# Splitting the scores of a half-step: one block of other TensorE work moved between the two groups of head pairs

## The chip, the cores and the metric

The kernel runs on one core of one Trainium2 chip. The metric is the device time of one execution in microseconds; the times shown are medians of several executions. Profile times are microseconds from the start of the profiled span.

## What is computed

A recurrent block and a stack of six local attention layers run on the same normalised input, and their product is added to the input. Cut to what matters here:

```python
for i in range(DEPTH):                      # 6 layers, x is (2, 1024, 128)
    x = attn_layer(shift_tokens(x), Wqkv[i], q_scale[i], k_scale[i], Wo[i]) + x
    x = ffn_layer(shift_tokens(x), ln_g[i], ln_b[i], W1[i], b1[i], W2[i], b2[i]) + x

# attn_layer: 16 heads of 64, l2-normalised and rotated q and k, windows of 32 tokens
sim = jnp.einsum('bhwie,bhwje->bhwij', bq, bk2) * QK_SCALE      # the scores
attn = jax.nn.softmax(jnp.where(mask, -big, sim), -1)
out = jnp.einsum('bhwij,bhwje->bhwie', attn, bv2)

# ffn_layer: xn is the layer norm of its input
hg = xn @ W1 + b1                           # the up product, 341 values and 341 gates
a, gate = jnp.split(hg, 2, -1)
return a * jax.nn.gelu(gate, approximate=False) @ W2 + b2

# outside: x + recurrent(layernorm(x)) * silu(attention stack(layernorm(x)))
```

## The kernel before

The two sequences of the batch are two streams, b = 0 and b = 1. The 1024 tokens of a stream are eight tiles of 128, and six layers of eight tiles make 48 steps. Each step has two half-steps, one per stream. The steps are written out one after the other, and each engine has its own function `half(i, b)` that lists what it does in half-step (i, b), strictly in that order; engines meet through semaphores alone.

The work is a software pipeline: in step i the projections (`qkv`) are those of tile i, the transposes of queries and keys and the scores are those of tile i-1, the softmax's probabilities, their product with the values and the output projection those of tile i-2, and the feed-forward part's up product that of tile i-4. Its normalised rows are transposed (`transpose_rows`) for tile i-3. In the last steps (40 to 47) the recurrent branch runs along. After step 47 a drain with an order of its own finishes what is under way.

TensorE writes to banks of PSUM in rings of two: `ps_qn` for projections, `ps_tr` for transposes, `ps_pv` for everything that leads to outputs (products with values, output projection, up and down products). A fill may start when the bank's last content has been read (`ring_free`), and `qn_order`, `tr_order`, `pv_order` give the order of fills in each ring. The scores of a half-step have one tile of their own, `ps_s`: `mask` (L833) writes the mask first, `scores(i, b, 0)` adds those of head pairs 0 to 3 and `scores(i, b, 1)` those of pairs 4 to 7 (L851), and the last matmul tells VectorE (`s_full`). Each `scores` call is 32 products; in the trace each is two matmuls, so 64 a call and 128 a half-step. They use 64 rows and 32 columns of the array at a time. `probs_v` (L872) uses 128 rows and 64 columns, everything else here 128 by 128.

At the end of a half-step TensorE does the value projections `qkv(i, b, (4, 5))` (L786 to L788), then, for b = 0, `ffn_up(i, 2)`, the third of three chunks of the up product (L922 to L924, six matmuls of 85 columns), or, for b = 1, `transpose_rows(i)` (L763, two transposes), and then the two `scores` calls. The next half-step begins with `transpose_probs` (L798), two projections, the output projection (L904, with the down product L884 for b = 1) and `transpose_keys` (L811).

On the other engines the steps that follow are these. ScalarE, in order at the end of half 0: `ffn_gelu(i, 2)` (L1232), `evac_v(i, 0, 5)` (L1240), a load of function tables, then in half 1 `evac_probs` (L1145), `inverse_root` (L1199, L1203), `square` (L1157), `evac_probs`, `square`. At the end of half 1: `evac_v`, `evac_rows` (L1129), `inverse_root`, `evac_probs`. VectorE: `ffn_gate(i, 2)` (L1647) and `mid_variance`, then `maxima` (L1547) and `less_max` (L1555) on the scores, and `rotate` (L1521, L1524), which waits for the square of the same bank and frees the bank. GpSimd's Newton steps for the norms wait for `inverse_root`, and it adds and scales queries and keys.

`ffn_up` and `transpose_rows` wait for nothing that `scores` makes, and the reverse:

Of the kernel before, what the change touches and what calls it, by code (L numbers as in the profile page):

```python
# [91 lines left out]
def valid(step):  # L92

    return not step.fixed or 0 <= step.n < STEPS
# [269 lines left out]
def layers(nc, a, x, xmid, branch, ident, eps_col, w, rec):  # L364

    with ExitStack() as ctx:
# [141 lines left out]
        def in_pair(r):  # L508

            return ps_pv[(r + 1) % 2], slice(LEAD + (2 + 2 * r) * P, LEAD + (4 + 2 * r) * P)  # L510
# [8 lines left out]
        def wait_fill(eng, sems, order, i, what):  # L519
            if exists(order, i, what):  # L520
                bank, n = fill(order, i, what)
                eng.wait_ge(sems[bank], n)
# [28 lines left out]
        with nc.Block() as block:  # L551
# [188 lines left out]
            def _(pe):  # L740
# [5 lines left out]
                def transpose_mixed(i, b):  # L746

                    t, s = next_tile(i, b)
                    if not valid(t):
                        return  # L750
                    bank, n = fill(tr_order, i, ("mixed", b))
                    ring_free(pe, tr_done, bank, n)
                    pe.wait_ge(x_shifted[t.n % 2], SHIFT_DMAS * (t.n // 2 + 1))
                    tr(ps_tr[bank][:, 0:P], x[:, s, t.tile, MIXED], ident[:, :]).then_inc(tr_full[bank], 1)

                def transpose_rows(i):
                    if not valid(i - 3):
                        return
                    bank, n = fill(tr_order, i, "rows")
                    ring_free(pe, tr_done, bank, n)  # L760
                    pe.wait_ge(normed, (i - 3).n + 1)
                    for s in range(B):
                        last = tr(ps_tr[bank][:, s * P:(s + 1) * P], normal[:, s, :], ident[:, :])  # L763
                    last.then_inc(tr_full[bank], 1)
# [6 lines left out]
                def qkv(i, b, chunks):  # L771
                    if not valid(i):
                        return
                    if 0 in chunks:
                        pe.wait_ge(xs_ready[b], i.n + 1)
                    if not first_half(i, b):
                        pe.wait_ge(lo_ready[chunks[0] // 2], (i.layer + 1) * w.splits(chunks[0] // 2))
                    for c in chunks:
                        if first_half(i, b):

                            part = c // 2
                            pe.wait_ge(*((lo_ready[part], w.splits(part)) if c % 2 else (lo_ready[part], 1) if part == 2 else (first_low, part + 1)))
                        bank = next_bank(i, ("qkv", b, c))
                        place = w.split_place(i.layer, c // 2, c % 2)
                        part = slice(place, place + COLS)
                        mm(ps_qn[bank][:, :], xs_hi[b][:, :], w_hi[:, part], start=True, stop=False)  # L786
                        mm(ps_qn[bank][:, :], xs_hi[b][:, :], w_lo[:, part], start=False, stop=False)  # L787
                        mm(ps_qn[bank][:, :], xs_lo[b][:, :], w_hi[:, part], start=False, stop=True).then_inc(qn_full[bank], 1)  # L788

                def transpose_probs(i, b, f):  # L790
                    j = i - 2
                    if not valid(j):
                        return
                    pe.wait_ge(probs_ready[b], j.n + 1)
                    bank, n = fill(tr_order, i, ("probs", b, f))
                    ring_free(pe, tr_done, bank, n)
                    for m in range(4):
                        last = tr(ps_tr[bank][:, m * P:(m + 1) * P],  # L798
                                  pr[b][:, 4 * f + m, :, :].rearrange("p u k -> p (u k)"), ident[:, :])
                    last.then_inc(tr_full[bank], 1)  # L800
# [14 lines left out]
                def transpose_keys(i, b):  # L815
                    transpose_qk(i, b, 2)
                    transpose_qk(i, b, 3)
# [18 lines left out]
                def scores(i, b, f):  # L836
                    j = i - 1
                    if not valid(j):
                        return
                    if j.first:  # L840
                        pe.wait_ge(cleared, 1)
                    if f == 0:
                        for k in (2, 3):
                            wait_fill(pe, tr_done, tr_order, i, ("qk", b, k))
                    wait_fill(pe, tr_done, tr_order, i, ("qk", b, f))
                    for hp in range(4 * f, 4 * f + 4):
                        for w in range(WINDOWS):
                            q = slice(WINDOW * w, WINDOW * (w + 1))
                            for h in range(2):
                                rows = slice(DH * h, DH * (h + 1))  # L850
                                last = mm(ps_s[q, h, hp, :], qT[rows, hp, q], kT[b][rows, hp, WINDOW * w:WINDOW * (w + 2)],  # L851
                                          start=False, stop=hp == HP - 1)
                    if f == 1:
                        last.then_inc(s_full, 1)
# [37 lines left out]
                def out_projection(i, b):  # L892
                    if not has_out(i, b):
                        return
                    bank = next_pv_bank(i, ("out", b))
                    if b == 0 and i.n < STEPS and valid(i - 4):
                        last = down_chunks(i, bank)
                    j = i - 2 - b
                    if valid(j):
                        pe.wait_ge(wo_in, (j.layer + 1) * 16)  # L900
                        for f in range(2):
                            wait_fill(pe, pv_done, pv_order, j + 2, ("pv", b, f))
                        for n in range(HP):
                            last = mm(ps_pv[bank][:, 0:P], oT[:, n // 2, n % 2, :], wo[:, n, :], start=(n == 0), stop=(n == HP - 1))  # L904
                    last.then_inc(pv_full[bank], 1)
# [82 lines left out]
                def transpose_input(columns, bank):  # L988
                    for n, c in enumerate(columns):
                        pe.wait_ge(s_xn, c + 1)  # L990
                        tr(bank[:, n * P:(n + 1) * P], in_tile(c), ident[:, :]).then_inc(s_tr, 1)

                def transpose_pair(r):

                    pe.wait_ge(s_xT, 2 + r)
                    transpose_input(range(HEAD * (r + 1), HEAD * (r + 2)), in_pair(r)[0])

                def half(i, b):
                    transpose_probs(i, b, 0)
                    transpose_probs(i, b, 1)  # L1000
                    qkv(i, b, (0, 1))
                    if (i.n, b) == (1, 1):
                        transpose_pair(1)
                    out_projection(i, 1 - b)
                    transpose_keys(i, b)
                    if b == 0:
                        probs_v(i, b, 0)
                        probs_v(i, b, 1)
                    qkv(i, b, (2, 3))
                    if b == 1:  # L1010
                        probs_v(i, b, 0)
                        probs_v(i, b, 1)
                    if i.first and b == 0:
                        pe.wait_ge(s_xT, 1)
                        transpose_input(range(B, HEAD), ps_pv[0])
                    transpose_mixed(i, b)
                    mask(i, b)
                    rec_hidden(i, b)
                    rec_gate_projection(i, b)
                    if (i.n, b) == (1, 1):  # L1020
                        transpose_pair(2)
                    transpose_qk(i, b, 0)
                    rec_output(i, b)
                    rec_rates(i, b)
                    transpose_qk(i, b, 1)
                    if b == 0:
                        ffn_up(i, 0)
                        ffn_up(i, 1)
                    qkv(i, b, (4, 5))
                    if (i.n, b) == (1, 0):  # L1030
                        transpose_pair(0)
                    if b == 0:
                        ffn_up(i, 2)
                    else:
                        transpose_rows(i)
                    scores(i, b, 0)
                    scores(i, b, 1)

                pe.wait_ge(s_const, 16)
# [1219 lines left out]
```

## Time and profile before

| | |
|---|---|
| median of 3 runs | 1588.56 us |
| lowest and highest | 1585.72, 1589.36 us |
| the profiled execution | 1589.05 us |
| its span | 1587.3 us |
| granted TensorE clock, mean | 0.989 |
| TensorE busy | 95% (matmuls), 83% (weight loads, beside them) |
| VectorE, ScalarE, GpSimd busy | 80%, 85%, 81% |

Busy shares are of the span. A matmul's duration overlaps the next one's, so the distance between starts is what one costs; in a merged row "x128" the second figure is the time from the first start to the last end. "Idle before" is time in which the engine did nothing ahead of the row, with what ended it; "issue" means that it waited for nothing that the profile shows. A table of stretches counts every instruction that runs in a stretch, those that began before it too.

### The profile page before, as it was taken

How to read it: one execution, taken by the hardware profiler on the slowest of the kernel's cores; microseconds unless marked ns; L12 is line 12 of the kernel's file. 1: busy time of each engine (PE TensorE's matmuls, PEld its weight loads, DVE VectorE, ACT ScalarE, POOL GpSimd, SP SyncE). 2: the span in 40 equal slices, each digit the busy share in tenths (PEclk: the TensorE clock that was granted, in tenths of full speed). 3: DMA queues.
4: the chain of work that ended last, by engine and by line, in shares of the span. 5: the costliest groups of instructions: out<-in, count | busy, mean ns of one | idle time of the engine just before them, and what ended most of it. 6: DMA issues, size and time to landing. Idle time of an engine off the chain costs nothing.

```text
span 1587.3 us, 64246 instructions
## 1 busy us (share of the span) xinstructions
PE 1504.4 (95%) x26159; PEld 1311.9 (83%) x26159; DVE 1277.5 (80%) x2033; ACT 1349.4 (85%) x2600; POOL 1291.7 (81%) x1268
## 2 busy tenths in 40 slices
PE   5899998999999999999999999999999999999965
PEld 3688887888888888888888888888888888888855
DVE  6888887887888788788878878888888888888845
ACT  5779888988988888898889888989998898999853
POOL 8899899788879888898887889888799777777710
PEclk8999999999999999999999999999999999999988
DMA  4345343444333354333344343344433333333231
GB/s 138 85 114 126 81 99 74 112 109 113 95 84 78 91 127 113 91 92 93 82 114 126 90 95 85 91 120 113 105 90 87 95 85 77 78 84 78 65 83 29
DMA packets 217811, 150.44 MB, mean 95 GB/s; under 512 B 144556, under 2 KB 164656, under 8 KB 217520
## 3 DMA queue, kind: packets, MB, share of 16 engines
q1 hardware_dynamic: 217520, 146.33, 38.0%
q8 instruction: 211, 3.46, 1.0%
q14 instruction: 80, 0.66, 0.1%
HBM read 27.50 MB, written 1.05 MB: 18 GB/s over the span
## 4 chain that ended last, share of the span: by engine, by line
PE 85%; issue 5%; POOL 4%; ACT 4%; DVE 2%; DMA 0%; SPq 0%; POOLq 0%; ACTq 0%; DVEq 0%
PE ps_pv L872 12%; PE ps_tr L811 10%; PE ps_pv L904 10%; PE ps_s L851 8%; PE ps_qn L786 8%; PE ps_qn L788 7%; PE ps_qn L787 7%; PE ps_tr L798 5%; PE ps_pv L884 4%; PE ps_s L833 2%; PE ps_pv L922 2%; PE ps_pv L924 2%; PE ps_pv L923 2%; POOL qk L1999 2%; ACT pbd L1145 1%
## 5 line engine op out<-in xcount | busy, mean ns | idle before, releaser
L1999 POOL TENSOR_TENSOR qk<-qk,t 128x1024 f32<-128x1024 f32 x192 | 459.6, 2394 | 6.8 <-DVE qk L1524 6.6
L2011 POOL TENSOR_TENSOR qkr<-qk,rinv 128x1024 f32<-128x1024 f32 x192 | 363.9, 1907 | 3.7 <-POOL rinv L1983 0.2
L1521 DVE TENSOR_TENSOR t<-ps_qn,tab 128x512 f32<-128x512 f32 x384 | 261.1, 680 | 101.5 <-ACT sq L1157 98.1
L786 PE MATMUL ps_qn<-w_hi,xs_hi 128*128 128x512 f32 x576 | 251.9, 437 | 11.7 <-DVE qk L1524 9.3
L1524 DVE TENSOR_TENSOR qk<-ps_qn,tab 128x512 f32<-128x512 f32 x384 | 261.3, 681 | 0.0
L1145 ACT ACTIVATE pbd<-ps_tr 64x512 f32<-64x512 f32 x384 | 225.7, 588 | 31.8 <-PE ps_tr L798 28.5
L1157 ACT ACTIVATE sq<-ps_qn 128x512 f32<-128x512 f32 x384 | 229.7, 599 | 25.9 <-PE ps_qn L788 17.1
L787 PE MATMUL ps_qn<-w_lo,xs_hi 128*128 128x512 f32 x576 | 228.6, 397 | 0.8 <-issue 0.8
L788 PE MATMUL ps_qn<-w_hi,xs_lo 128*128 128x512 f32 x576 | 228.9, 397 | 0.0
L811 PE MATMUL ps_tr<-ident,qkr 128*128 128x128 f32 x1536 | 213.2, 275 | 11.5 <-ACT pbd L1145 8.5
L1534 DVE TENSOR_REDUCE ss<-sq 128x32 f32<-128x2048 f32 x96 | 218.5, 2276 | 0.0
L811 PEld LDWEIGHTS ps_tr<-ident,qkr 128*128 128x128 f32 x1536 | 176.4, 142 | 41.6 <-issue 26.1
L872 PEld LDWEIGHTS ps_pv<-pbd,v_win 128*64 128x64 f32 x6144 | 187.5, 138 | 27.6 <-issue 27.5
L872 PE MATMUL ps_pv<-pbd,v_win 128*64 128x64 f32 x6144 | 200.7, 224 | 2.2 <-ACT pbd L1145 2.2
L2021 POOL TENSOR_TENSOR pr<-pr,rrec 128x1024 f32<-128x1024 f32 x96 | 183.5, 1911 | 11.5 <-DVE rrec L1571 11.5
L904 PE MATMUL ps_pv<-wo,oT 128*128 128x128 f32 x1536 | 188.9, 276 | 3.8 <-DVE oT L1541 3.8
L904 PEld LDWEIGHTS ps_pv<-wo,oT 128*128 128x128 f32 x1536 | 184.2, 193 | 8.3 <-issue 2.1
L1547 DVE TENSOR_REDUCE rmax<-ps_s 128x16 f32<-128x1024 f32 x96 | 117.1, 1220 | 84.6 <-PE ps_s L851 82.6
L851 PE MATMUL ps_s<-kT,qT 64*32 64x64 f32 x12288 | 154.5, 226 | 14.4 <-issue 14.3
L851 PEld LDWEIGHTS ps_s<-kT,qT 64*32 64x32 f32 x12288 | 136.3, 105 | 34.2 <-issue 33.1
L786 PEld LDWEIGHTS ps_qn<-w_hi,xs_hi 128*128 128x128 f32 x576 | 109.4, 190 | 38.3 <-issue 11.6
L1969 POOL TENSOR_SCALAR floored<-ss 128x34 f32<-128x34 f32 (+1 forms) x96 | 30.2, 315 | 128.4 <-DVE ss L1603 113.6
(176 smaller groups left out, 3019.8 us busy)
## 6 DMA issues: line engine op xcount, KB each, us to landing
v_win<-v_new SPq DMA_DIRECT2D x576, 128.0 KB
v_win<-v_new SPq DMA_DIRECT2D x192, 64.0 KB
v_win<-v_win SPq DMA_DIRECT2D x188, 64.0 KB, 2.0
kT<-kT SPq DMA_DIRECT2D x84, 128.0 KB, 3.0
w_raw<-in_Wqkv SPq DMA_DIRECT2D x18, 512.0 KB, 3.9
rot<-in_rot SPq DMA_DIRECT2D x48, 128.0 KB
wo<-in_Wo SPq DMA_DIRECT2D x6, 512.0 KB, 4.8
x<-x SPq DMA_DIRECT2D x48, 56.0 KB
```

The costliest lines, as they stand in the source:

```text
L786: mm(ps_qn[bank][:, :], xs_hi[b][:, :], w_hi[:, part], start=True, stop=False)
L787: mm(ps_qn[bank][:, :], xs_hi[b][:, :], w_lo[:, part], start=False, stop=False)
L788: mm(ps_qn[bank][:, :], xs_lo[b][:, :], w_hi[:, part], start=False, stop=True).then_inc(qn_full[bank], 1)
L811: last = tr(ps_tr[bank][:, m * P:(m + 1) * P], qkr[b][:, (4 * f + m) * P:(4 * f + m + 1) * P], ident[:, :])
L851: last = mm(ps_s[q, h, hp, :], qT[rows, hp, q], kT[b][rows, hp, WINDOW * w:WINDOW * (w + 2)], start=False, stop=hp == HP - 1)
L872: last = mm(pv_target(bank, hp, w), v_win[b][:, w, hp * DH:(hp + 1) * DH], pbd[:, hp, :, WINDOW * w:WINDOW * (w + 1)], start=True, stop=True)
L904: last = mm(ps_pv[bank][:, 0:P], oT[:, n // 2, n % 2, :], wo[:, n, :], start=(n == 0), stop=(n == HP - 1))
L1145: last = f(pbd[rows, 4 * k:4 * k + 4, h, :], ps_tr[bank][rows, :].rearrange("p (m t) -> p m t", m=4), ACT.Copy)
L1521: v.tensor_tensor(t2[:, part].rearrange("p (h s d) -> p h s d", s=2, d=DH // 2), swapped, tab[:, 2 * k + 1:2 * k + 2, :].rearrange("p o (s ...
L1524: v.tensor_tensor(qk[b][:, part].rearrange("p (h d) -> p h d", d=DH), ps_qn[bank][:, :].rearrange("p (h d) -> p h d", d=DH), tab[:, 2 * k: ...
L1999: g.tensor_tensor(qk[b][:, part], qk[b][:, part], t2[:, part], ALU.add).then_inc(added[b], 1)
L2011: g.tensor_tensor(qkr[b][:, part].rearrange("p (h d) -> p h d", d=DH), qk[b][:, part].rearrange("p (h d) -> p h d", d=DH), rinv[b][:, k * ...
```

## The change

In TensorE's `half`, the call `scores(i, b, 0)` moves from behind the branch to ahead of it. So the third chunk of the up product (b = 0) or the transposes of the normalised rows (b = 1) now stand between the scores of head pairs 0 to 3 and those of pairs 4 to 7. No instruction is added or taken away, and the order of fills in every ring stays. The drain is as it was.

```diff
                     qkv(i, b, (4, 5))
                     if (i.n, b) == (1, 0):
                         transpose_pair(0)
+                    scores(i, b, 0)
                     if b == 0:
                         ffn_up(i, 2)
                     else:
                         transpose_rows(i)
-                    scores(i, b, 0)
                     scores(i, b, 1)
```

## Rows read from the trace of the kernel before

**Rows 1.** The page: busy time of each engine, and the instruction packets of queue 8.
```profile
PE 1504.4 (95%) x26159; PEld 1311.9 (83%) x26159; DVE 1277.5 (80%) x2033; ACT 1349.4 (85%) x2600; POOL 1291.7 (81%) x1268
...
q8 instruction: 211, 3.46, 1.0%
```

**Rows 2.** Table of stretches: start:end, length, busy time and count, clock, DMA.
```profile
130.00:1495.00 1365.00, 1336.94 (x23533) 1174.28 (x23532) 1124.21 (x1755) 1214.17 (x2324) 1160.78 (x1133) 1.00 0.40 95
```

**Rows 3.** Waits, 130 to 1495 us: total us, times, longest us.
```profile
DVE rmax L1547 <- PE ps_s L851: 72.6, 32, 3.7
...
PE ps_s L851 <- issue: 10.6, 9, 1.6
...
PE ps_tr L798 <- issue: 8.1, 6, 1.8
...
PE ps_tr L811 <- ACT pbd L1145: 5.6, 7, 1.1
...
PEld ps_qn L786 <- DVE qk L1524: 2.1, 5, 0.4
```

**Rows 4.** Order of time, TensorE, end of an even half: start, us, instruction.
```profile
746.38 0.40 PE L788 MATMUL ps_qn<-w_hi,xs_lo 128*128 128x512 f32 x1
746.62 0.28 PE L922 MATMUL ps_pv<-fxn_hi,w_hi 128*85 128x256 f32 x1
...
747.20 0.28 PE L924 MATMUL ps_pv<-fxn_hi,w_lo 128*85 128x256 f32 x1
747.41 1.59 PE L851 MATMUL ps_s<-kT,qT 64*32 64x64 f32 x128
```

**Rows 5.** Table of stretches, L851 alone: 64 scores, then the rest; best row.
```profile
762.18:762.80 0.62, 0.62 (x64) 0.62 (x67) 1.00 0.91 205
762.80:763.56 0.76, 0.76 (x91) 0.76 (x72) 1.00 0.66 189
...
883.26 1.48 PE L851 MATMUL ps_s<-kT,qT 64*32 64x64 f32 x128
```

**Rows 6.** Order of time, TensorE, second step, which has no block there.
```profile
83.56 0.40 PE L788 MATMUL ps_qn<-w_hi,xs_lo 128*128 128x512 f32 x1
83.89 1.68 PE L851 MATMUL ps_s<-kT,qT 64*32 64x64 f32 x128
```

**Rows 7.** Order of time, TensorE, from L872's pieces to a projection.
```profile
799.82 0.93 PE L872 MATMUL ps_pv<-pbd,v_win 128*64 128x64 f32 x26
800.68 0.50 PE L786 MATMUL ps_qn<-w_hi,xs_hi 128*128 128x512 f32 x1
801.01 0.40 PE L787 MATMUL ps_qn<-w_lo,xs_hi 128*128 128x512 f32 x1
801.25 0.39 PE L788 MATMUL ps_qn<-w_hi,xs_lo 128*128 128x512 f32 x1
```

**Rows 8.** Order of time, TensorE, end of an odd half.
```profile
761.64 0.39 PE L788 MATMUL ps_qn<-w_hi,xs_lo 128*128 128x512 f32 x1
761.87 0.38 PE L763 MATMUL ps_tr<-ident,normal 128*128 128x128 f32 x2
762.18 1.58 PE L851 MATMUL ps_s<-kT,qT 64*32 64x64 f32 x128
```

**Rows 9.** Order of time, ScalarE, VectorE and TensorE, after the third up chunk.
```profile
747.52 0.47 ACT L1232 ACTIVATE hid<-ps_pv,b 85x256 f32<-85x256 f32 x1 [0.28 <-PE ps_pv L924]
...
753.23 0.60 ACT L1157 ACTIVATE sq<-ps_qn 128x512 f32<-128x512 f32 x1
...
764.21 0.23 ACT L1199 ACTIVATE log_ss<-floored 128x32 f32<-128x32 f32 x1 [0.62 <-POOL floored L1969]
...
754.47 0.68 DVE L1524 TENSOR_TENSOR qk<-ps_qn,tab 128x512 f32<-128x512 f32 x1
...
755.95 0.40 PE L786 MATMUL ps_qn<-w_hi,xs_hi 128*128 128x512 f32 x1
```

**Rows 10.** Order of time, TensorE, first step of the second layer.
```profile
242.59 0.63 PE L811 MATMUL ps_tr<-ident,qkr 128*128 128x128 f32 x4 [1.07 <-ACT pbd L1145]
```

## The prediction

> **What bounds the kernel now.** I read the page first: TensorE is busy for 1504.4 of 1587.3 us, more than any other engine [rows 1]. An average over the run can mislead, so the second view is a table of one long stretch: from 130 to 1495 us, where the layers repeat, TensorE is busy for 1336.9 of 1365 us at the full granted clock [rows 2]. The third is the list of what TensorE waited for in that stretch [rows 3]: 18.7 us in 15 pauses are "issue" (nothing that the profile shows was missing), 5.6 us are waits for ScalarE's copies of the probabilities, 2.1 us for VectorE's rotations. So time put onto TensorE is paid almost in full, and a result that comes later for another engine costs nothing until its slack is gone. The fourth view is TensorE's own order at the place of the edit, one matmul after the other [rows 4 to 8]. The profiled execution took 1589.05 us (span 1587.3 and 1.75 around it), 0.5 above the median 1588.56; I sum against 1589.05 and take off 0.5 at the end.
>
> **Part 1: the array changes shape twice more.** The scores run on 64x32 pieces of the array, everything beside them in this half-step on 128x128. Before, the scores of a half-step are one unbroken row of 128 matmuls; after, they are two rows of 64 with the moved block between.
> Even half (stream 0; the block is the six matmuls of the third up product). Before, by starts: last value product 746.38, first up 746.62 (0.24), last up 747.20 (0.58), first score 747.41 (0.21) [rows 4]; the first 64 scores take 0.62 [rows 5]. Sum 1.65 us, then the second 64.
> After: from value product to scores the second step, which has no up product yet, shows the price: 83.56 to 83.89, 0.33 [rows 6]. First 64 scores: 0.61 to the last start. From scores to up product is nowhere in the trace. Nearest is the change from L872 (128x64 pieces) to a projection: L872's row ends at 800.75, one lasts 0.22, so the last began at 800.53 and the projection at 800.68, 0.15 later; and the second projection matmul starts 0.33 after the first where 0.24 is usual, another 0.10 [rows 7]. So 0.15, then the block in 0.68, and 0.21 back into the scores. Sum 1.98 us, difference **+0.33 us**. The bounds of the unseen change are 0.02 (no cost beyond the scores' own pitch) and 0.25 (all of it); I take 0.25, as L872 is the same kind of change.
> Odd half (stream 1; the block is two transposes): before, value product to transposes 0.23, between them 0.11, into the scores 0.20, first scores 0.62, in all 1.16 [rows 5, 8]; after 0.33, 0.61, 0.15, then 0.16 (half of the extra, as a transpose loads less) and 0.20, in all 1.45. Difference **+0.29 us**.
> The Trainium skill speaks against the change here: TensorEngine Tiling, Key Properties, says that changing the tiling mode drains the engine. It gives no price; TensorE: Matmul & The Clock Gate, in its step on the drain, has about 128 cycles, which at 2.4 GHz makes an estimate of 0.05 us a change, 9.5 us for two changes in 89 half-steps. The trace agrees that a change costs, and shows more: about 0.09 going in and 0.25 coming out.
>
> **Part 2: what the interruption gives back.** The first 64 scores take 0.62 us, the second 64 take 0.76 in this ordinary half-step [rows 5]; in the best one the whole row is 1.48 instead of 1.58, all of it in the second 64 [rows 5, 8]. The engine enters the scores with instructions queued and runs short of them later. With a block of 0.5 to 0.9 us between, the second 64 start as the first do: 0.76 becomes about 0.63, **-0.13 us** a half-step. Bounds: nothing, and -0.15.
> The up product exists in steps 4 to 47 (44), the row transposes in 3 to 47 (45); the drain has its own list and is untouched. 44 x (0.33 - 0.13) + 45 x (0.29 - 0.13) = 8.8 + 7.2 = **+16.0 us**.
>
> **Part 3: the long pauses.** Fifteen half-steps have an "issue" pause of 0.8 to 1.8 us near the end of the scores (nine) or in the transposes just behind (six), 18.7 us in all [rows 3]. TensorE's 52,318 instructions come in 211 packets, one for about 248 [rows 1], and the scores with their weight loads use up 256 in 1.5 us. If such a pause ends when a packet has arrived, what is spent ahead of it is time in which the packet travels, and those half-steps get no longer: 6 x 0.20 + 9 x 0.16 = **-2.6 us**. Runtime: NRT & Kernel Launch, Instruction fetch mechanics, in the Trainium skill, also has blocks of 256 instructions, fetched while the one before runs, and calls the crossing mostly hidden; hidden, it would absorb nothing and 16.0 would stand. The 15 pauses speak against "hidden" in this kernel.
>
> **Part 4: later hand-overs.** The up product ends 1.98 - 0.21 - 0.82 = 0.95 us later. ScalarE's GELU waits for it already (idle 0.28) [rows 9], and behind it in order stand the copy of v, a table load, the copies of the probabilities, the root that GpSimd's Newton step waits for, and the two squares that VectorE's rotations wait for. All shift by 0.95, TensorE itself by 0.20, so 0.75 of slack is used up. The second square ends at 753.83, its rotation at 755.15; the bank is taken by the projection at 755.95 [rows 9]. Slack 0.80 less some 0.05 for a hand-over: just enough. The row transposes end 0.85 us later; ScalarE loses about 0.55 there and idles 0.62 soon after for GpSimd [rows 9], which covers it. Where slack is nil it is paid: at a layer's last step VectorE has one more cast in this chain and TensorE waits for the last rotation (5 waits, 2.1 us) [rows 3]; at a layer's first step it waits for the copy of the probabilities (1.07 us) [rows 10]. Five layer ends: 5 x 0.75 + 5 x 0.55 = 6.5 us. Some six more half-steps without slack in the first steps and beside the recurrent branch: 6 x 0.2 = 1.2. **+7.7 us**, bounds 0 and, if half of the even steps pay 0.3 more, 14. No DMA is issued or moved past by these steps; the scores as a whole end 0.2 later, for which VectorE waits in 32 of the half-steps with time to spare (72.6 us idle) [rows 3].
>
> Sum: 16.0 - 2.6 + 7.7 = +21.1; 1589.05 + 21.1 - 0.5 = **1609.6 us**.
>
> **Rivals.**
> Supply (faster): the gaps around the scores are no change of shape but TensorE's instructions running short, so that leaving the scores costs nothing with a slow block behind, and the long pauses shrink. Each half-step then pays 0.09 for going in and gets 0.13 back, -3.6 us, and half of the 18.7 us goes too: -13, **1576 us**. For it: the pauses are "issue". Against it: the same 0.15 stands behind L872. It decides once coming out costs under 0.04. Chance 0.07.
> Other engines set the pace (no difference): if TensorE would wait for banks anyway, 0.2 more is hidden, **1589 us**. For it: ScalarE is busy for 85% and has an unbroken chain through the odd half. Against: TensorE's waits on other engines come to about 8 us in 1365 [rows 3]. Chance 0.07.
> Slack gone everywhere (slower still): if the shift is a little over the rotation's 0.75 us of slack in all even steps, each pays 0.3 to 0.4 more: 21 + 44 x 0.35 = +36, **1625 us**. It decides at a shift of 0.75. Chance 0.12.
>
> **How the numbers follow.** Forecast 0.74, around 1609.6; its own bounds are 1598 (no hand-over waits, coming out 0.2 instead of 0.25) and 1621 (no gain in the second 64). The range runs from 1598 to 1624, to the edge of the last rival, and leaves out the first two and the tails. Chances: faster by over 0.2% (3.2 us, about what a measurement of this kernel can tell from none) 0.07; within 0.2% 0.08; slower 0.85.
>
> **What the changed profile would show.** Scores in rows of 64, twice a half-step; 0.33 from value product to scores; 0.15 from scores to block, and the up block at 0.68 by starts; the second 64 at 0.63. Still about 15 long pauses at the same places, each 0.2 shorter. GELU of the third chunk idle 1.2 instead of 0.28. Longer waits for the last rotation and the probabilities at layer ends alone. The prediction is wrong if coming out costs under 0.1 us, if the second 64 still take 0.76, or if such waits show up in ordinary steps.

## The result, and the profile after

| | before | after |
|---|---|---|
| median (4 runs each, same chip) | 1587.14 us | 1611.55 us |
| lowest and highest | 1582.6, 1589.36 | 1610.09, 1612.24 |
| the profiled execution | 1589.05 us | 1612.24 us |
| its span | 1587.3 us | 1610.5 us |

The changed kernel is slower: ratio 1.0156, 95% interval 1.0131 to 1.0181. The forecast was 1609.6 us.

The page of the kernel after, first the busy times (against [rows 1]), then three groups of the costliest. The instruction counts are those of before: nothing was added, and TensorE is busy 29 us longer for the same work.
```profile
PE 1533.4 (95%) x26159; PEld 1304.3 (81%) x26159; DVE 1282.5 (80%) x2033; ACT 1344.2 (83%) x2600; POOL 1289.8 (80%) x1268
...
L851 PE MATMUL ps_s<-kT,qT 64*32 64x64 f32 x12288 | 169.6, 225 | 14.8 <-issue 14.7
L1547 DVE TENSOR_REDUCE rmax<-ps_s 128x16 f32<-128x1024 f32 x96 | 117.1, 1220 | 76.2 <-PE ps_s L851 75.9
...
L1232 ACT ACTIVATE hid<-ps_pv,b 128x256 f32<-128x256 f32 x144 | 68.4, 475 | 80.6 <-PE ps_pv L924 80.4
```

Waits of the kernel after from 130 to 1520 us (25 us more than for before, since the same layers last longer): TensorE's matmuls, then its weight loads, then ScalarE. Against [rows 3]:
```profile
PE ps_s L851 <- issue: 12.1, 15, 1.5
PE ps_tr L811 <- ACT pbd L1145: 6.0, 6, 1.1
PE ps_tr L798 <- issue: 1.4, 4, 0.5
PE ps_pv L872 <- DVE x L1577: 1.1, 2, 0.5
...
PEld ps_qn L786 <- DVE qk L1524: 9.3, 34, 0.4
...
ACT hid L1232 <- PE ps_pv L924: 56.5, 43, 1.8
```
The engines behind TensorE wait more for it. TensorE's matmuls wait hardly more for them, and its weight loads a little: 9.3 us for the rotations, where [rows 3] has 2.1. So its own row of instructions has become longer, as said. Order of time, TensorE, end of an even half (against [rows 4]) and of an odd half (against [rows 8]):
```profile
751.17 0.40 PE L788 MATMUL ps_qn<-w_hi,xs_lo 128*128 128x512 f32 x1
751.50 0.86 PE L851 MATMUL ps_s<-kT,qT 64*32 64x64 f32 x64
752.29 0.35 PE L922 MATMUL ps_pv<-fxn_hi,w_hi 128*85 128x256 f32 x1
752.48 0.28 PE L923 MATMUL ps_pv<-fxn_lo,w_hi 128*85 128x256 f32 x1
...
752.94 0.28 PE L924 MATMUL ps_pv<-fxn_hi,w_lo 128*85 128x256 f32 x1
753.15 0.41 PE L851 MATMUL ps_s<-kT,qT 64*32 64x64 f32 x20
754.04 0.69 PE L851 MATMUL ps_s<-kT,qT 64*32 64x64 f32 x44 [0.47 <-issue]
...
767.37 0.40 PE L788 MATMUL ps_qn<-w_hi,xs_lo 128*128 128x512 f32 x1
767.70 0.86 PE L851 MATMUL ps_s<-kT,qT 64*32 64x64 f32 x64
768.49 0.44 PE L763 MATMUL ps_tr<-ident,normal 128*128 128x128 f32 x2
768.85 0.86 PE L851 MATMUL ps_s<-kT,qT 64*32 64x64 f32 x64
769.64 1.12 PE L798 MATMUL ps_tr<-ident,pr 128*128 128x128 f32 x8
```
Value product to scores is 0.33 (751.17 to 751.50, 767.37 to 767.70). The up block spans 0.65 by starts (752.29 to 752.94), the second matmul 0.19 behind the first where 0.12 is usual. The odd half takes 2.27 us from the last value product to L798 (767.37 to 769.64). Before it was 2.06, from the 761.64 of [rows 8] to the next row of that view:
```profile
763.70 1.09 PE L798 MATMUL ps_tr<-ident,pr 128*128 128x128 f32 x8
```

**Where the time went.** I summed the distances between the starts of TensorE's matmuls in both traces, from the first projection of step 3 to that of step 47, sorted by place. "Stretch" is what lies between the last value product and L798. "Pause" is any distance over 0.4 us in it; behind even halves all that L798's distances changed by is counted with the pauses, because some pauses there shrink below 0.4. The window holds 43 of the 44 changed even halves and 44 of the 45 odd ones.

| place | after less before |
|---|---|
| stretch from the last value product to L798, even halves, without pauses | +10.1 us |
| the same, odd halves | +10.7 |
| pauses in it, and at L798 behind even halves | -4.0 |
| fourth projection of odd halves, which takes the bank that the second rotation frees | +2.5 |
| L872: two ends of layers +1.3, other steps +0.5 | +1.8 |
| L984, a product of the recurrent branch | +0.9 |
| all the rest | +0.3 |
| sum | +22.3 |

The profiled executions differ by 23.2 us, so this table holds nearly all of it. The medians of the distances show what the 10.1 and the 10.7 consist of (us, start to start):

| | before | after |
|---|---|---|
| value product to what follows | 0.231 to 0.234 | 0.327 |
| scores to block | - | 0.147 |
| up block, first to last | 0.586 | 0.654 |
| transposes, first to second | 0.108 | 0.165 |
| block to scores | 0.209 even, 0.201 odd | 0.209, 0.203 |
| all scores, first to last of each row | 1.369 | 2 x 0.642 |
| sum, even half (with 0.147 to L798) | 2.55 | 2.77 |
| sum, odd half | 2.06 | 2.27 |

A new round trip between the shapes costs 0.30 us, and two rows of 64 win back only 0.085 of the scores' own 1.369.

One reading was missed ahead of the prediction. That the scores are left for full-size work is in the kernel before as well, at the end of each half-step: from the last score to L798 it is 0.147 us (median of the 88 half-steps of the window), and L798's second transpose starts 0.165 behind the first, where 0.109 is usual. These are the two figures that the changed kernel shows at the row transposes, so the price of leaving could have been read there and not estimated.

### The profile page after: what moved, and what is told of

Read it like the earlier page. It is cut to its first block, busy times and chain, and to the rows that moved or that the text cites. A ratio compares the mean times of both kernels' runs of the same rounds, so it can differ in the third digit from the quotient of the medians.

```text
span 1610.5 us, 64246 instructions
## 1 busy us (share of the span) xinstructions
PE 1533.4 (95%) x26159; PEld 1304.3 (81%) x26159; DVE 1282.5 (80%) x2033; ACT 1344.2 (83%) x2600; POOL 1289.8 (80%) x1268
## 4 chain that ended last, share of the span: by engine, by line
PE 85%; POOL 5%; issue 4%; ACT 3%; DVE 2%; DMA 0%; SPq 0%; POOLq 0%; ACTq 0%; DVEq 0%
PE ps_pv L872 11%; PE ps_tr L811 10%; PE ps_pv L904 9%; PE ps_s L851 9%; PE ps_qn L786 8%; PE ps_qn L788 7%; PE ps_qn L787 7%; PE ps_tr L798 5%; PE ps_pv L884 4%; PE ps_pv L922 3%; PE ps_s L833 2%; POOL qk L1999 2%; PE ps_pv L924 2%; PE ps_pv L923 2%; POOL qkr L2011 1%
## 5 line engine op out<-in xcount | busy, mean ns | idle before, releaser
L811 PE MATMUL ps_tr<-ident,qkr 128*128 128x128 f32 x1536 | 212.7, 275 | 11.2 <-ACT pbd L1145 8.2
L872 PEld LDWEIGHTS ps_pv<-pbd,v_win 128*64 128x64 f32 x6144 | 190.1, 139 | 28.9 <-issue 28.4
L811 PEld LDWEIGHTS ps_tr<-ident,qkr 128*128 128x128 f32 x1536 | 175.8, 141 | 40.8 <-issue 25.2
L872 PE MATMUL ps_pv<-pbd,v_win 128*64 128x64 f32 x6144 | 203.9, 225 | 3.0 <-ACT pbd L1145 1.9
L851 PEld LDWEIGHTS ps_s<-kT,qT 64*32 64x32 f32 x12288 | 136.7, 105 | 67.9 <-issue 51.6
L851 PE MATMUL ps_s<-kT,qT 64*32 64x64 f32 x12288 | 169.6, 225 | 14.8 <-issue 14.7
L1232 ACT ACTIVATE hid<-ps_pv,b 128x256 f32<-128x256 f32 x144 | 68.4, 475 | 80.6 <-PE ps_pv L924 80.4
```

What stands on the lines that cost most here:

```text
L811: last = tr(ps_tr[bank][:, m * P:(m + 1) * P], qkr[b][:, (4 * f + m) * P:(4 * f + m + 1) * P], ident[:, :])
L872: last = mm(pv_target(bank, hp, w), v_win[b][:, w, hp * DH:(hp + 1) * DH], pbd[:, hp, :, WINDOW * w:WINDOW * (w + 1)], start=True, stop=True)
```

## The experiments

Every kernel ran beside the kernel before on its chip, and each ratio is to that. "Pauses" are TensorE's waits named "issue" at the scores and at L798, from 130 to 1495 us; the kernel before has 18.7 us of them [rows 3].

**One half at a time.** In the first kernel only the even half is changed, in the second only the odd one:
```diff
                     if b == 0:
+                        scores(i, b, 0)
                         ffn_up(i, 2)
                     else:
                         transpose_rows(i)
-                    scores(i, b, 0)
+                        scores(i, b, 0)
                     scores(i, b, 1)
```


> Only the even half is changed: the third up product stands between the two calls of scores, the odd half is as before. Theory A (each extra change of the array's shape is paid on TensorE, the later up product costs little): 44 half-steps at 0.24 us, about 2.5 us of waits for the second rotation, long pauses up to 1 us less; +12 us against before, 1599 us. Theory B (the hand-overs to ScalarE and VectorE cost most, and the up product is the one with the long chain behind it): this half carries nearly the whole +24, at least +18.


Measured: 1605.92 us, 1.0106 (1.0087 to 1.0125), by this ratio 16.8 us more than before. That lies between the two theories (+12, and at least +18).

> Only the odd half is changed: the transposes of the rows stand between the two calls of scores. Theory A (shape changes): 45 half-steps at 0.23 us less some 2 us of shorter long pauses, +8.5 us, 1596 us, and e1 and e2 add up to the whole change. Theory B (hand-overs): little is behind the row transposes in time, so +2 to +5 us.


Measured: 1597.42 us, 1.0061 (1.0042 to 1.008), 9.7 us more.

The sum of both, 26.5, stands against 24.8 for the whole (by its ratio): they add up. Without pauses the changed stretches are longer by 10.7 and by 10.2 us, each as in the whole change. The rest differs by what the shift does elsewhere. In the odd one the pauses shrink by 4.1 us. In the even one they shrink by 7.3, but the hand-overs cost more than in the whole change, some 9.6 us by starts: 4.2 at L811, where TensorE waits for the copies of the probabilities (7.7 us in 11 places, where [rows 3] has 5.6 in 7), 2.5 for the second rotation, 2.0 at L872 and 0.9 at L984. That lifts it above the +12 of theory A. The profiled execution, the fastest of its four, is only 13.9 us above the profiled one of before, so some 3 of the 16.8 stand in no trace. TensorE's waits of the kernel with the even half alone:
```profile
PE ps_s L851 <- issue: 11.1, 15, 1.5
PE ps_tr L811 <- ACT pbd L1146: 7.7, 11, 1.1
```

**Is it the shape or the interruption?** Here the normalised rows are transposed in pieces of the scores' own shape, 64 by 32. Both kernels leave out features 64 to 127 of those rows. One has the block ahead of the scores, as before, the other between them in the odd half; so the pair differs by an interruption without a change of shape. (In short; the drain keeps the full-size transposes.)
```diff
-    last = tr(ps_tr[bank][:, s * P:(s + 1) * P], normal[:, s, :], ident[:, :])
+    for q in range(WINDOWS):
+        to = slice(WINDOW * q, WINDOW * (q + 1))
+        last = mm(ps_tr[bank][to, s * P:(s + 1) * P], normal[0:DH, s, to], ident[0:DH, :], start=True, stop=True)
```


> Order of before, but in the steps the row transposes are eight products in 64x32 pieces of the array (the shape of the scores) over features 0 to 63 only; features 64 to 127 of the transposed rows become zero, which is left out work. It is the partner of e4. Against before: the change of shape now comes ahead of the block instead of behind it, the block itself takes 0.1 to 0.4 us by starts instead of 0.11; between -4 and +10 us.

> As e3, but with this block in 64x32 pieces between the two calls of scores in the odd half; even half as before. The same move as in e2, the rows are handed over as late, only the block has the scores' own shape (and again leaves out features 64 to 127). Theory A (shape changes): no additional change of shape, so within 2 us of e3. Theory B (the interruption of the scores or the later hand-over costs): e4 is longer than e3 by as much as e2 is longer than before, 8 to 10 us.


Measured: 1599.08 us, 1.0064 (1.0046 to 1.0083), and 1600.73, 1.0074 (1.0058 to 1.0091). The pair lies 1.65 us apart, where the same move with full-size transposes cost 9.7; the two intervals overlap for the most part, and of the two profiled executions the second is the shorter one, by 1.2. The traces say more: without pauses the odd stretch is 5.2 us shorter with the interruption (why, no run shows), where it is 10.2 longer in the kernel with only the odd half changed. Against that stand 3.5 us in the transposes of the probabilities behind the odd half, whose fifth now starts 0.22 behind the fourth instead of 0.11, and 0.9 us of longer pauses. So the interruption by itself does not make TensorE's row longer: the change of shape does. In the trace of the second, in order of time, scores (L857 here) and pieces (L769) run into each other:
```profile
761.12 0.86 PE L857 MATMUL ps_s<-kT,qT 64*32 64x64 f32 x64
761.78 0.48 PE L769 MATMUL ps_tr<-ident,normal 64*32 64x128 f32 x9
762.00 0.24 PE L857 MATMUL ps_s<-kT,qT 64*32 64x64 f32 x1
```
The scores' last start to the next block is 0.017 us here (median), and 0.147 with a block of another shape. (The pieces are more matmuls, so both kernels are dearer than before, the first by a little more than the +10 us that were its upper bound; only their distance is read. The pieces also load smaller weights than a full-size transpose, so "shape" here means both.)

**The long pauses.** Eight or twenty transposes that nobody reads, ahead of everything else, shift where the blocks of instructions end:
```diff
                 pe.wait_ge(s_const, 16)
+                for _ in range(8):
+                    tr(ps_pv[0][:, 0:P], ident[:, :], ident[:, :])
                 for b in range(B):
```


> The kernel before with eight more 128x128 transposes (16 instructions) at the very start of TensorE's program, about 1 us of work. Nothing else moves, but every later instruction stands 16 places further on in the stream of instruction packets. Theory A (a long pause is TensorE waiting for its next packet of 256 instructions, and it comes only when a packet's end falls in a few places at the end of the scores): in the kernel before, the pauses end once the packet's end has drifted to matmul 104 of the odd scores; 8 further on from the start the packet's end is at 104 from the beginning, most of the 15 pauses are gone, -12 to -18 us plus 1, about 1573 us. Theory B (the pauses come from data, banks or DMA traffic at that time): they stay, +1 us.


Measured: 1573.9 us, 0.9905 (0.9885 to 0.9924). Sixteen instructions more, and the kernel is 17 us faster by the medians. TensorE's waits, against [rows 3]:
```profile
PE ps_tr L811 <- ACT pbd L1147: 6.7, 8, 1.1
PE ps_s L851 <- issue: 3.3, 2, 1.7
PE ps_tr L798 <- issue: 1.1, 1, 1.1
```
18.7 us of pauses have become 4.4.

> As e5 with twenty transposes more (40 instructions, about 2 us). Theory A (packets): the pauses leave their places, but a packet's end now falls 0 to 14 instructions behind the odd scores of every third step, in the transposes of probabilities, a place like that of the even halves' pauses; some 6 to 10 pauses there, between -12 and 0 us. Theory B: pauses where they were, +2 us.


Measured: 1582.92 us, 0.9954 (0.9937 to 0.997). With 40 instructions more the pauses come back at other half-steps, nine at L798, most of them behind the odd half's scores, and five in the scores; the longest, in order of time:
```profile
971.52 0.41 PE L798 MATMUL ps_tr<-ident,pr 128*128 128x128 f32 x2 [1.89 <-issue]
```
So a pause belongs to a place in the count of instructions, not to a place in the work. Both runs, with sixteen and with forty more, lie where the theory of the packets put them.

> The changed kernel with the eight transposes of e5 at the start. Theory A (packets and shape changes are separate): most of its 13.5 us of long pauses are gone, -9 to -13 us against the changed kernel, about 1600 us, and its distance to e5 is what the shape changes and hand-overs cost without any pauses, 23 + 4 = 27 us. Theory B (the split scores made the pauses shorter and that part is lost otherwise): distance to e5 20 us or less.


Measured: 1605.07 us, 1.0101 (1.008 to 1.0121). With the pauses mostly away on both sides the change costs 1605.07 - 1573.9 = 31 us, not 20 or less: the plain kernels hide part of its price. Of the 30.3 us between the two traces, 12.3 and 10.8 are the even and the odd stretch without pauses, 4.0 are new pauses in the even halves' scores, 2.7 the second rotation, 1.4 L872, 0.9 L984; at the transposes of the probabilities and elsewhere 1.8 are saved. Without pauses the distance is thus some 28 us, where 27 had been expected.

The traces of the kernel before and of the changed one show the mechanism. Four pauses of each inside the odd half's scores: the start of the matmul behind the pause (TensorE's records), how many scores of its row stand ahead of it, and how long before it the last block of instructions had set out (queue 8 of the DMA records):
```
before: 270.27  112 of 128  2.52      after: 272.44  48 of the second 64  2.81
        362.66  111         3.04             365.28  47                   2.94
        454.82  110         2.50             551.79  45                   2.47
        549.13  109         2.98             644.53  44                   2.44
```
It is the same instruction, 64 + 48 = 112, and from pause to pause it moves back by one, as the count drifts (at 46 the changed kernel has no pause over 0.4 us). The first of each, in order of time:
```profile
270.27 0.35 PE L851 MATMUL ps_s<-kT,qT 64*32 64x64 f32 x16 [0.82 <-issue]
```
```profile
272.44 0.35 PE L851 MATMUL ps_s<-kT,qT 64*32 64x64 f32 x16 [0.86 <-issue]
```
and the block ahead of the first, in the kernel before's DMA records from 267.6 to 268.0 us:
```profile
q8 instruction: 1, 0.02, 19.1%
```

**The hand-overs.** The changed kernel, but ScalarE copies the values ahead of the third GELU in even halves:
```diff
                     if b == 0:
+                        evac_v(i, b, 5)
                         ffn_gelu(i, 2)
-                    evac_v(i, b, 5)
```
(in short; two steps' extra calls keep their place ahead of `evac_v`, which odd halves have where it was)

> The changed kernel with one swap on ScalarE: in even halves the copy of the second value bank stands ahead of the GELU of the third chunk instead of behind it, so 0.58 us of work is done while ScalarE waits for the up product, and the chain behind it starts that much earlier. Theory A: the 2.5 us of waits for the second rotation and some of the 1.8 us at layer ends go, -3 us against the changed kernel, 1608 us. Theory B (the later chain costs more than the waits that TensorE shows, for example by using up all slack in front of pauses): -8 us or more.


Measured: 1607.06 us, 1.0112 (1.0091 to 1.0133), 4.5 us under the changed kernel's median and, by the ratios, which belong to two chips, 7. Its weight loads wait for the rotation
```profile
PEld ps_qn L786 <- DVE qk L1524: 1.7, 4, 0.4
```
instead of 9.3 us in 34 places, and by starts the rotation's 2.5 us, 0.8 of L872's and L984's 0.9 are back, 4.2 us in all. The hand-overs of the whole change are thus worth some 4 to 5 us, as the first theory has it; the traces show no 8 us or more.

**Two breaks in an odd half.** The rows' transposes one by one, behind pairs 0 and 1 and behind pairs 2 and 3:
```diff
                     else:
-                        transpose_rows(i)
-                    scores(i, b, 0)
+                        scores(i, b, 0, (0, 1))
+                        transpose_rows(i, (0,))
+                        scores(i, b, 0, (2, 3))
+                        transpose_rows(i, (1,))
                     scores(i, b, 1)
```


> As e2 (odd half alone), with one break more: head pairs 0 and 1, transpose of stream 0, pairs 2 and 3, transpose of stream 1, pairs 4 to 7. Theory A (each pair of shape changes has a price): a second break adds 0.2 to 0.25 us to 45 half-steps, +9 to +11 us over e2, so 18 to 20 over before, 1607 us. Theory B (one late hand-over of the rows is what costs): the rows are ready at the same time as in e2, so no more than e2's +10 us.


Measured: 1592.87 us, 1.0008 (0.9995 to 1.002): a miss. The breaks are there and the stretch is longer, 2.40 us from 756.20 to 758.60:
```profile
756.20 0.40 PE L789 MATMUL ps_qn<-w_hi,xs_lo 128*128 128x512 f32 x1
756.52 0.45 PE L852 MATMUL ps_s<-kT,qT 64*32 64x64 f32 x32
756.91 0.33 PE L763 MATMUL ps_tr<-ident,normal 128*128 128x128 f32 x1
757.17 0.45 PE L852 MATMUL ps_s<-kT,qT 64*32 64x64 f32 x32
757.55 0.33 PE L763 MATMUL ps_tr<-ident,normal 128*128 128x128 f32 x1
757.82 0.86 PE L852 MATMUL ps_s<-kT,qT 64*32 64x64 f32 x64
758.60 1.11 PE L799 MATMUL ps_tr<-ident,pr 128*128 128x128 f32 x8
```
but the pauses are down to 6.5 us. Splitting the calls adds waits to TensorE's program, so the count of its instructions had changed too. The control has the same calls without the breaks:
```diff
-                        scores(i, b, 0, (0, 1))
                         transpose_rows(i, (0,))
-                        scores(i, b, 0, (2, 3))
                         transpose_rows(i, (1,))
+                        scores(i, b, 0, (0, 1))
+                        scores(i, b, 0, (2, 3))
```


> The control of the run with two blocks in the odd half (1592.9 us, no slower than before). Here the calls are split as there, so the waits and the instructions are the same in number, but both transposes stand ahead of one unbroken row of scores, as before. Theory A: a change of shape has its price (two more round trips than before in an odd half, 0.35 us by the two traces, so 45 x 0.35 = 15.8 us), and that run was saved from it because other instruction counts let the long pauses fall from 18.7 to about 6.5 us. Then this kernel has the short pauses and no breaks: 1592 - 12 = 1580 us, and the run with two blocks stands 13 to 16 us above it. Theory B: the breaks cost nothing in an odd half (the time saved in the later scores pays for them). Then both kernels take the same 1593 us within 2 us. Theory C, a mixture: the pauses depend on the place of the scores too, so that they return here, about 18 us in 15 places; then the time says nothing of the shapes, and the stretches from the last value product to the next half-step have to be compared in the two traces.


Measured: 1583.93 us, 0.9953 (0.9937 to 0.997). The pair is 9 us apart by medians (12.5 by the profiled executions), not equal, and less than the 13 to 16 expected, since the control kept more pauses, 10.5 us:
```profile
PE ps_s L852 <- issue: 5.6, 6, 1.4
...
PE ps_tr L799 <- issue: 4.9, 5, 1.9
```
By starts, the odd stretch without pauses is 16.1 us longer with the breaks (0.37 in each of the 44 odd halves of the window, 0.345 by the medians), the pauses are 4.2 us shorter, and all else is within 1.3. So two breaks cost 0.35 to 0.37 us an odd half, and the miss came from comparing with a kernel whose instructions are counted otherwise.

**Two other orders.** The order of before with the eight transposes and the ScalarE swap:

> Order of the kernel before on TensorE, with e5's eight transposes at the start and e8's swap on ScalarE. If the two are independent: e5's -16 us and a little of e8's (TensorE waits less for rotations in the order of before, so at most -2 us): 1571 us, faster than both kernels. If packets and hand-overs share their slack, it is e5's time or a few us above.


Measured: 1571.67 us, 0.9867 (0.9848 to 0.9887), the fastest of all, 20 us under the kernel before and, by the medians, 40 under the changed one. TensorE's waits named issue:
```profile
PE ps_s L851 <- issue: 1.7, 1, 1.7
PE ps_tr L798 <- issue: 0.8, 1, 0.8
```
The step from 1573.9 to 1571.67 is 2.2 us, in another set of runs. By ratio the two are 0.9885 to 0.9924 and 0.9848 to 0.9887: that the swap helps without the change is likely, not certain.

The next puts the odd half's products with the values directly ahead of the scores, to save a shape change:
```diff
-                    if b == 1:
-                        probs_v(i, b, 0)
-                        probs_v(i, b, 1)
...
                     else:
                         transpose_rows(i)
+                        probs_v(i, b, 0)
+                        probs_v(i, b, 1)
                     scores(i, b, 0)
```
(ScalarE's copies of the products and the order of fills follow)

> e10 with the probabilities' product with the values (L872, 128x64 pieces) of the odd half moved from behind the third and fourth projection to directly ahead of the scores, and its copies on ScalarE to the end of the half-step. Theory A (shape changes): into L872 and out of it costs 0.09 and 0.2 us where it stood; beside the scores one of the two changes goes, -0.2 us in 46 half-steps, -9 us against e10, 1562 us. Theory B (TensorE's packets of instructions): 384 instructions in 3.3 us without slow work between bring more and longer pauses, and the later copies hold up the probabilities of the next half-step; 0 to +15 us against e10.


Measured: 1622.32 us, 1.0182 (1.0151 to 1.0214), 50 us more than the kernel it was made from: a miss. A new wait stands where the products used to be. Order of time, TensorE, and its waits:
```profile
768.92 0.63 PE L811 MATMUL ps_tr<-ident,qkr 128*128 128x128 f32 x4 [0.89 <-ACT xs_hi L1119]
...
771.10 2.08 PE L872 MATMUL ps_pv<-pbd,v_win 128*64 128x64 f32 x64
773.11 1.11 PE L851 MATMUL ps_s<-kT,qT 64*32 64x64 f32 x92
```
```profile
PE ps_tr L811 <- ACT xs_hi L1119: 31.8, 36, 0.9
PE ps_s L851 <- issue: 14.0, 16, 1.2
```
The query transposes need the bank of the mixed tile, and the 2 us of L872 had covered ScalarE's way to its copies. The shape change was not saved either: L872's row ended its starts about 0.15 us before the scores, as ahead of any other shape. The 31.8 us are the largest part of the 50 and the pauses have grown by 13; by starts, 7.6 us more stand at L984 and 5.6 at the fifth projection of odd halves. The rest I have not accounted for piece by piece.

## Why the prediction was right, point by point

The direction, the mechanism and the time held (1609.6 for 1611.55). The sum came out partly by luck, because errors cancelled: the stretches cost 5 us more than forecast, the pauses and the hand-overs together nearly 4 less. The medians moved by 24.4 us, from 1587.14 to 1611.55, the traces by the 22.3 that are split up here:

| term | forecast | measured by starts |
|---|---|---|
| stretches, parts 1 and 2 | +16.0 | +20.9 |
| pauses, part 3 | -2.6 | -4.0 |
| hand-overs, part 4 (and all the rest) | +7.7 | +5.4 |
| sum | +21.1 | +22.3 |

**Part 1, shapes.** Going in 0.33, coming out 0.15, back 0.21 and 0.20: as read from [rows 4, 6 to 8]. The extra in the block behind was taken as 0.10 for the up block and 0.05 for the transposes; it is 0.07 and 0.06. So 0.30 in both halves for +0.33 and +0.29. L872 was a good stand-in for the change to a projection, though the row from the scores to L798 would have given 0.147 and 0.165 directly. That a transpose loads less, the reason given for halving the extra, no run tests. The Trainium skill (TensorEngine Tiling (Array Packing), Key Properties) states that a change of the tiling mode drains the engine. The runs agree that such a change has a price, 0.2 us a break with one and none that shows without one; that the price is a drain they do not show. The estimate of 0.05 us from the drain step of the Trainium skill's TensorE: Matmul & The Clock Gate is a third of the 0.147 that leaving the scores takes.

**Part 2, what the break gives back**, is the term that was mis-sized: 0.13 a half-step forecast, 0.085 measured by medians and 0.064 by the mean that the sums leave ((26.5 - 20.9) / 87, with 26.5 the shapes' 0.30 to 0.31 in the 87 half-steps of the window), so 4 to 6 us too much over 89. The second 64 did get shorter, to 0.64 from 0.76 by the one half-step of [rows 5], which is 0.744 by the median of all. But the first 64 got longer, from 0.61 to 0.64, since each row ends with four slower starts (17 ns, where about 8 is usual), and now two rows end. I had read the first 64 off a stretch cut out of a longer row, and such a stretch lacks the end. Why the starts slow down along a row no run shows; that the engine runs short of queued instructions, as the prediction has it, stays a guess.

**Part 3, pauses.** The sum had the right size (-4.0 for -2.6), the picture was half right. "About 15, in the same places, each 0.2 shorter" holds for those in the odd half's scores: nine as before, seven of them at the same instruction, 2.4 us less in all. It does not hold for the even halves. There the six at L798, 9.7 us between starts, have shrunk by 6.8, and six new ones in the second row of the scores (the one at 754.04 among them) take 5.2. What decides is the count of instructions at which a block ends, as the runs with 16 and 40 more show. The Trainium skill (Runtime: NRT & Kernel Launch, Instruction fetch mechanics) calls the crossing mostly hidden; in this kernel some 15 of 211 show, and moving them was worth 17 us of 1591.

**Part 4, hand-overs**, had its size from the wrong place. I gave 6.5 us to layer ends, 1.2 to six steps at the start and beside the recurrent branch, and nothing to ordinary steps. Layer ends took 1.3, at two of them (a wait for the bank that VectorE's L1577 frees, 0.5 us each), and the rotation of the even half, where I had put 0.80 of slack against 0.75 of shift and called it just enough, took 2.5 us in small pieces, in 34 waits of its weight loads. My own bound (a shift a little over the slack) was the more exact picture; it stayed small because the shift just reached the slack. By the prediction's own list such waits in ordinary steps were a sign of being wrong, and for this part they are: the wait was placed wrongly and its size came out by luck. The wait of the GELU came as said: forecast 1.2, in the row
```profile
753.26 0.47 ACT L1232 ACTIVATE hid<-ps_pv,b 85x256 f32<-85x256 f32 x1 [1.22 <-PE ps_pv L924]
```

**The rivals.** Supply: coming out costs 0.15, far over the 0.04 from which it decides; its second half, that the supply of instructions is worth more than ten microseconds, is true, but by another lever than this change. Other engines: a longer row of TensorE's was paid nearly in full. Slack gone everywhere: the even steps' rotation waits average 2.5 / 44 = 0.06 us, not 0.35.

**Not settled.** Whether the 0.147 behind the scores is a drain of the small pieces or the time in which the first weights of the other shape are loaded: no run separates the two. Nor why a second break in the odd half costs less (0.37 for two, 0.24 for one), though by starts the value product's 0.10 is paid only once, and single transposes pay no 0.165 between them but 0.26 instead of 0.20 ahead of the next scores.

## What to carry to other kernels

Keep work that uses the array in small pieces in one unbroken row: each time it is parted by work of full size costs some 0.30 us in starts and gives back 0.06 to 0.09, and 89 such places made 1.3% of this kernel. Before a difference of a per cent is put down to an order of work, run the same order with a few instructions more or less; here 16 instructions moved the time by about 1%, two thirds of what the change itself did. When a block is moved, ask whose slack it was covering: the products with the values were 2 us of cover for a copy, and moving them cost 50 us.

## What was not expected of the hardware

- Sixteen TensorE instructions added at the start made the kernel 17 us faster (1590.9 to 1573.9), and 40 gave half of that. In the traces of the kernel before and the changed one, each long pause ends 2.2 to 3.1 us after a block of instructions (16 KB, 211 in all) has set out.
- Parting a row of scores by matmuls of the same shape in 45 places changed the time by 1.65 us, within the noise, and made TensorE's own stretch 5.2 us shorter; by another shape it cost 9.7 us, 0.2 each.
- The first 64 of a long row of scores start in 0.61 us, the second 64 in 0.744 (median). Rows of 32 that end by themselves take 0.238 each, and rows of 64 take 0.642.
